# The adding stage of a two-layer metaformer: one block-diagonal product per pair of images, three sets of buffers, long runs, no loops

## The reference, cut to what matters

```python
probs = softmax(x @ gate_w.T + gate_b, axis=1)            # over the tokens of an image
vals, idx = top_k(probs.transpose(0, 2, 1), 8)            # 8 tokens per image and expert
topv, topi = vals.transpose(0, 2, 1), idx.transpose(0, 2, 1)
gathered = take_along_axis(x, topi.reshape(B, 8 * E)[:, :, None], axis=1).reshape(B, 8, E, D)
pooled = einsum('bked,bke->bed', gathered, topv)
h = gelu(einsum('ebd,edh->ebh', [pooled, 1], weight1))
out = einsum('ebh,eho->ebo', [h, 1], weight2)             # one row of 128 per image and expert
weighted = einsum('beo,bke->bkeo', out, topv)
outputs = zeros.at[b, topi].add(weighted)                 # added back to the chosen tokens
x = x + outputs
```

## Time and profile before

| | us |
|---|---|
| median of 3 executions | 14604.2 (14583.66 to 14649.89) |
| the profiled execution, its own time | 14537.58 |
| its span, first to last instruction | 14535.8 |
| mean granted TensorE clock in it | 0.810 of full speed |
| routing, experts, adding in the span | 11718 to 13396, to 13704, to 14535.8 |

### The profile page before, as it was taken

The page is one execution under the profiler, slowest core; times in us unless marked ns, Lnnn a source line. Parts: engine busy times, 40 slices in busy tenths (PEclk is TensorE's granted clock), DMA queues, the critical chain, the costliest instruction groups (busy, mean ns, idle before and its releaser), DMA issues. The chain is left out here.

```text
span 14535.8 us, 248087 instructions
## 1 busy us (share of the span) xinstructions
PE 11419.5 (79%) x87538; PEld 8744.4 (60%) x87538; DVE 11053.6 (76%) x22880; ACT 9833.3 (68%) x22679; POOL 4012.8 (28%) x3975
## 2 busy tenths in 40 slices
PE   7888888888888867777777777777777547776998
PEld 5666666666666645555555555555555235555888
DVE  6777777777777718999999999999999965554133
ACT  6888888888888846666666666667666567776100
POOL 5444444445444421212111211112121111211000
PEclk9999999999999967777777777777777677777555
DMA  3333333333333321111111111111111133333599
GB/s 69 86 81 82 81 82 87 76 90 73 90 77 86 75 61 41 53 53 53 51 47 52 53 53 53 51 46 53 53 52 40 23 84 94 99 90 89 172 316 309
DMA packets 1967708, 1189.72 MB, mean 82 GB/s; under 512 B 48853, under 2 KB 1900056, under 8 KB 1958436
## 3 DMA queue, kind: packets, MB, share of 16 engines
q1 hardware_dynamic: 1554148, 967.87, 26.3%
q10 hardware_dynamic: 408832, 205.55, 5.0%
q0 software_dynamic: 3648, 2.20, 0.1%
HBM read 708.85 MB, written 466.62 MB: 81 GB/s over the span
## 5 line engine op out<-in xcount | busy, mean ns | idle before, releaser
L1236 PEld LDWEIGHTS s_pW<-s_XU,s_vh 128*128 128x128 f32 x6272 | 1415.7, 261 | 1969.1 <-ACT s_XU L1107 1699.7
L1236 PE MATMUL s_pW<-s_XU,s_vh 128*128 128x64 f32 x6272 | 1493.2, 331 | 1071.4 <-ACT s_XU L1107 1071.4
L1107 ACT ACTIVATE s_XU<-s_pW,s_zb 128x64 f32<-128x64 f32 x3136 | 995.7, 318 | 1788.7 <-PE s_pW L1236 1738.1
L1265 PE MATMUL s_pG<-s_wg,s_XNT 128*128 128x384 f32 (+1 forms) x3200 | 1506.0, 559 | 37.5 <-ACT s_Z L1086 37.5
L832 POOL TENSOR_TENSOR s_rst<-s_var,s_epst 128x16 f32<-128x16 f32 (+1 forms) x100 | 141.7, 1417 | 3906.6 <-DVE s_var L79 3906.6
L408 ACT ACTIVATE KB<-pV,qkb 32x392 f32<-32x392 f32 x2048 | 1190.5, 581 | 25.0 <-PE pV L498 1.1
L248 POOL TENSOR_TENSOR SS<-SS,mx 128x784 f32<-128x784 f32 x512 | 769.5, 1503 | 804.8 <-DVE mx L341 804.6
L1203 PEld LDWEIGHTS s_pY<-s_hident,s_XU 128*128 128x128 f32 (+1 forms) x3200 | 752.2, 305 | 177.7 <-issue 129.6
L1711 PE MATMUL c_pS<-c_OX,c_Wm 64*112 64x128 f32 x3584 | 737.6, 420 | 91.1 <-DVE c_X L1727 76.6
L460 ACT ACTIVATE XH<-XR,nm,rs 112x128 f32<-112x128 f32 x1792 | 733.6, 485 | 92.1 <-POOL nm L267 83.6
L506 PE MATMUL pS<-KB,QT 128*64 128x196 f32 x8192 | 793.7, 336 | 0.0
(11 more groups left out here) (249 smaller groups left out, 31958.3 us busy)
## 6 DMA issues: line engine op xcount, KB each, us to landing
XL<-in_x_dram SPq DMA_DIRECT2D x64, 1568.0 KB, 12.4
XR<-in_x_dram SPq DMA_DIRECT2D x64, 1568.0 KB, 18.0
x_dram<-XR SPq DMA_DIRECT2D x64, 1568.0 KB, 8.1
xh_dram<-XH SPq DMA_DIRECT2D x64, 1568.0 KB, 8.1
r_X<-x_dram SPq DMA_DIRECT2D x64, 1568.0 KB, 14.2
c_X<-x_dram SPq DMA_DIRECT2D x64, 1568.0 KB, 19.4
out_dram<-c_X ACTq DMA_DIRECT2D x64, 1568.0 KB, 13.9
s_XQ<-xh_dram ACTq DMA_DIRECT2D x384, 256.0 KB, 2.8
```

The costliest lines, as they stand in the source:

```text
L1107: act.activation(XU[j % 2][:, t, :], pW[t // R % 2][:, B * (t % R):B * (t % R) + B], ACT.Tanh, bias=zb[:, 0:1], scale=0.5).then_inc(u_sb, 1)
L1236: pe.matmul(pW[t // R % 2][:, B * (t % R):B * (t % R) + B], vh[:], before, start=False, stop=True, skip_group_check=True).then_inc(z_ps, 1)
L1265: pe.matmul(pG[i % 3][0:tc, 0:3 * C], XNT[:, i, 0:tc], wg[:], start=True, stop=True).then_inc(g_ps, 1)
```

## The change

- In the adding stage both images of a pair share one product: 128 rows deep, 256 columns wide. OX becomes [128, 2, 128], with image 0's rows in the upper left block and image 1's in the lower right; the two other blocks are set to zero once, and the loads fill only their own blocks. A PSUM bank then holds two pieces of 112 tokens for both images, and VectorE's addition writes both images' X. There are 14 banks per pair, as before.
- X and Wm have three sets (NL = 3), allocated ahead of the experts. `load_pair` fills them; SP calls it in the experts' code at e = 8, 16 and 24 for pairs 0, 1 and 2, and afterwards in the adding stage. OX keeps two sets and is loaded there.
- Partition t now holds tokens t*NT + n, 28 tokens one after the other, so that a partition's run in DRAM is 28 x 512 = 14,336 bytes, in routing's loads, in the loads of the adding stage and in the stores of the output. The mask's order of tokens follows.
- Both stages are written out, without loops.
- Both images of a pair are stored when the whole pair is done.

```diff
@@ routing @@
-            with eng.Fori(0, (NP - 4) // 2) as i:
-                body(Image(i * 2 + 2, i + 1, 0), True, True, True)
-                body(Image(i * 2 + 3, i + 1, 1), True, True, True)
-            body(Image(NP - 2, NP // 2 - 1, 0), True, True, True)
+            for m in range(2, NP - 1):
+                body(Image(m, m // 2, m % 2), True, True, True)
...
-                                         .rearrange("a (n t) c -> t (a n) c", t=T)).then_inc(x_ld[n.par][o], 16)
+                                         .rearrange("a (t n) c -> t (a n) c", t=T)).then_inc(x_ld[n.par][o], 16)
@@ ahead of the experts @@
+        NL = 3
...
+        X = [sb(f"X{p}", [T, 2, NT, C]) for p in range(NL)]
+        Wm = [sb(f"Wm{p}", [P, S]) for p in range(NL)]
...
+        def load_pair(eng, m):
+            p = m % NL
+            eng.dma_start(Wm[p][:], wm_d[m]).then_inc(w_ld[p], 16)
+            for o in range(2):
+                eng.dma_start(X[p][:, o], x3_d[2 * m + o:2 * m + o + 1, :, :].rearrange("a (t n) c -> t (a n) c", t=T)
+                              ).then_inc(x_ld[p], 16)
@@ experts, SP, after the load of W2[e] @@
+                    if e in (8, 16, 24):
+                        load_pair(sp, e // 8 - 1)
@@ adding, SP @@
-                def body(m):
-                    wait(sp, s_ps, (m.idx - 1) * 2 * NG)
-                    sp.dma_start(Wm[m.par][:], ...)
-                    sp.dma_start(OX[m.par][:], ...)
-                    wait(sp, o_st[m.par], m.half * 32)
-                    for o in range(2):
-                        sp.dma_start(X[m.par][o][:], ...)
+                sp.wait_ge(zero, 1)
+                for m in range(NP):
+                    p = m % 2
+                    wait(sp, s_ps, (m - 1) * NU)
+                    for o in range(2):
+                        sp.dma_start(OX[p][E * o:E * o + E, o, :], ox_d[2 * m + o]).then_inc(ox_ld[p], 16)
+                    if m >= 1 and m + NL - 1 < NP:
+                        wait(sp, s_ps, m * NU)
+                        wait(sp, o_st[(m - 1) % NL], ((m - 1) // NL + 1) * 32)
+                        load_pair(sp, m + NL - 1)
@@ adding, ScalarE's queue @@
+                for m in range(NP):
+                    act.wait_ge(s_sb, m * NU + NU)
+                    for o in range(2):
+                        act.dma_start(out[2 * m + o:2 * m + o + 1, :, :].rearrange("a (t n) c -> t (a n) c", t=T),
+                                      X[m % NL][:, o]).then_inc(o_st[m % NL], 16)
@@ adding, TensorE @@
-                                w = pe.matmul(bank[0:T, C * t:C * t + C], Wm[m.par][E * o:E * o + E, T * n:T * n + T],
-                                              OX[m.par][E * o:E * o + E, :], start=True, stop=True)
+                for m in range(NP):
+                    pe.wait_ge(w_ld[m % NL], m // NL * 16 + 16)
+                    pe.wait_ge(ox_ld[m % 2], m // 2 * 32 + 32)
+                    for u in range(NU):
+                        i = m * NU + u
+                        wait(pe, s_sb, i - 3)
+                        for n in range(2):
+                            w = pe.matmul(pS[i % 4][0:T, 2 * C * n:2 * C * n + 2 * C],
+                                          Wm[m % NL][:, T * (2 * u + n):T * (2 * u + n) + T],
+                                          OX[m % 2][:].rearrange("p o c -> p (o c)"), start=True, stop=True)
+                        w.then_inc(s_ps, 1)
@@ adding, VectorE @@
+                for p in range(2):
+                    dve.memset(OX[p][0:E, 1, :], 0.0)
+                    w = dve.memset(OX[p][E:P, 0, :], 0.0)
+                w.then_inc(zero, 1)
+                for m in range(NP):
+                    dve.wait_ge(x_ld[m % NL], m // NL * 32 + 32)
+                    for u in range(NU):
+                        i = m * NU + u
+                        v = X[m % NL][:, :, 2 * u:2 * u + 2, :].rearrange("t o n c -> t n o c")
+                        dve.wait_ge(s_ps, i + 1)
+                        dve.tensor_tensor(v, pS[i % 4][0:T, :].rearrange("t (n o c) -> t n o c", n=2, o=2), v,
+                                          ALU.add).then_inc(s_sb, 1)
```

More of the change, by code:

```diff
@@ L1556, in expert_phase, with sb, sem @@
         NH4 = HID // P
+        NL = 3
+        def sb(name, shape, dt=F32):
+            return ctx.enter_context(nc.sbuf_tensor("c_" + name, shape, dt))
+        def sem(name):
+            return ctx.enter_context(nc.semaphore("c_" + name))
+        X = [sb(f"X{p}", [T, 2, NT, C]) for p in range(NL)]
+        Wm = [sb(f"Wm{p}", [P, S]) for p in range(NL)]
+        x_ld = [sem(f"x_ld{p}") for p in range(NL)]
+        w_ld = [sem(f"w_ld{p}") for p in range(NL)]
+        def load_pair(eng, m):
[4 more added lines that the diff above has]
+                              ).then_inc(x_ld[p], 16)
         with ExitStack() as ex:
@@ L1652, in sem @@
                 return sc.enter_context(nc.semaphore("c_" + name))
-            X = [[sb(f"X{p}{o}", [T, NT, C]) for o in range(2)] for p in range(2)]
-            Wm = [sb(f"Wm{p}", [P, S]) for p in range(2)]
-            OX = [sb(f"OX{p}", [P, C]) for p in range(2)]
+            OX = [sb(f"OX{p}", [P, 2, C]) for p in range(2)]
             pS = [ps(f"pS{a}", [P, 512]) for a in range(4)]
-            x_ld = [[sem(f"x_ld{p}{o}") for o in range(2)] for p in range(2)]
-            w_ld = [sem(f"w_ld{p}") for p in range(2)]
+            zero = sem("zero")
+            ox_ld = [sem(f"ox_ld{p}") for p in range(2)]
             s_ps = sem("s_ps"); s_sb = sem("s_sb")
[L1661 to L1669, removed]
+            o_st = [sem(f"o_st{p}") for p in range(NL)]
+            NU = NT // 2
             block = sc.enter_context(nc.Block())
@@ L1697, in _ @@
[L1697 to L1698 removed]
+                        act.dma_start(out[2 * m + o:2 * m + o + 1, :, :].rearrange("a (t n) c -> t (a n) c", t=T),
+                                      X[m % NL][:, o]).then_inc(o_st[m % NL], 16)
+                for p in range(NL):
+                    act.wait_ge(o_st[p], len(range(p, NP, NL)) * 32)
             @block.tensor
             def _(pe):
[L1702 to L1713 removed]
@@ L1715, in _ @@
-                each(body, pe)
+                for m in range(NP):
[9 more added lines that the diff above has]
+                        w.then_inc(s_ps, 1)
@@ L1717, in _ @@
             @block.vector
             def _(dve):
-                def body(m):
-                    for o in range(2):
-                        dve.wait_ge(x_ld[m.par][o], m.half * 16 + 16)
-                        for k in range(NG):
-                            i = (m.idx * 2 + o) * NG + k
-                            bank = pS[(o * NG + k) % 2 + 2 * m.par]
-                            v = X[m.par][o][:, GT * k:GT * k + GT, :].rearrange("t n c -> t (n c)")
-                            dve.wait_ge(s_ps, i + 1)
-                            dve.tensor_tensor(v, bank[0:T, :], v, ALU.add).then_inc(s_sb, 1)
@@ L1729, in _ @@
-                each(body, dve)
+                for p in range(2):
[10 more added lines that the diff above has]
+                                          ALU.add).then_inc(s_sb, 1)
```

18 lines of the change are left out of this document (removed).

## The result

| | before | after |
|---|---|---|
| median of 17 executions | 14608.2 us (14565.5 to 14649.9) | 14661.6 us (14625.7 to 14679.8) |
| ratio, 95% interval | | 1.0039 [1.0031, 1.0047] |
| profiled execution, its span | 14537.6, 14535.8 | 14660.2, 14658.4 |

The kernel is 0.4% slower. That lies within the 0.5% called no change ahead of the run, but with 17 executions on either side the interval excludes 1. It is 212 us over the forecast of 14450 and outside its range.

The account below looks back on a forecast made before the run. TensorE, transfers and the two-set ring were taken to bound the adding stage together, near 25.7 us per pair, with DMA the bound afterwards. 14604 - 161 (adding) + 6 (experts) + 0 (routing) = 14449, stated as 14450; range 14385 to 14575.

Parts of the forecast that it names:

- I take 401 for all of it: Adding stage: all transfers in long runs move at 401 GB/s, so two pairs take 40.4 us.
- Rival B: Adding stage: transfers stay at 345 GB/s because loads and stores share the engines; 47.5 us per two pairs, 14531; chance 0.10.
- I take 42 per two pairs: Adding stage: SP's queue chain takes 39 us, the DMA engines 40.4; interleaving imperfectly, 42 per two pairs.
- The products: Adding stage: 128-row depth brings TensorE's clock up; 12.3 us per pair, 14.8 if it starts low.
- the forecast of 671: Adding stage: start, first two bursts, 15 turns of 42 us and the end sum to 671 us against 832.
- Rival A: Adding stage: TensorE's clock stays at 0.50, bursts 23.9 us, stage 785, kernel 14564; chance 0.14.
- Loads among the experts: Experts: three early load points each make the following weights 2 us late, +6 us; bounds 0 and 12.
- Routing at 0: Routing: earlier X and removed loops cost 0; its rhythm may move +-40 us, none expected.
- Perhaps ten more slow pairs: Routing: the median's 66.6 us over the profiled execution of the kernel before comes from perhaps ten more slow pairs.
- C: Adding stage: long runs in both directions disturb each other; at 281 GB/s or less the kernel is 0.5% slower; chance 0.05.
- D: Routing and adding: instruction fetches of unrolled code stall TensorE, +189 us, kernel 14638; chance 0.03.
- The sum: Whole kernel: 14604 less 161 in the adding stage plus 6 in the experts gives 14449, stated as 14450.

Follow-up runs that it names:

- e6: Kernel after, with X loaded into 128 partitions of 28 tokens (1792 KB per image, rows not the right tokens): 14638.2 us in one execution, adding stage 824.
- e5: Kernel after, with each image of X loaded in two transfers, to partitions 0 to 63 and 64 to 111: ratio 1.0151, adding stage 983 us.
- e8: Kernel before, with 14,336-byte runs in routing's loads and the adding stage's loads and stores: ratio 0.9972, adding stage 793 us.
- e2: Kernel after, with X and the output moved in 512-byte pieces again: ratio 1.0088, adding stage 897 us.
- e3: Kernel after, with OX issued ahead of the next load_pair and its wait for a store: ratio 1.0015, adding stage 828 us.
- e7: Kernel before, with routing's pairs written out without a loop, nothing else changed: ratio 1.0003, routing 1753 us.
- e10: Kernel before, unedited, profiled a second time: 14603.8 us in one execution, routing 1743.
- e11: Kernel before, with pairs on 128 partitions, 64 x 64 quarter products, three sets, spread early loads, all OX loaded at the start: ratio 0.9849, adding stage 595 us.
- e12: Kernel after, with OX issued ahead as in e3 and the first three pairs' nine loads spread among the experts: ratio 0.9999, adding stage 814 us.
- e13: Kernel after, with the edits of e12 and the 128-partition loads of e6 together (rows not the right tokens): ratio 0.9916, adding stage 705 us.

## Why the prediction was wrong, step by step

Two steps failed: the bandwidth of the loads, and the time of the chain. The first alone would have made the stage some 770 us (41 + 15 x 48.5, an estimate from the rate below). The second held it at 824 even where the loads were fast (e6).

**"I take 401 for all of it."** It held for the stores (24.6 bytes per ns of one engine) and fell for the loads of X, 40% of all bytes: they go into 112 partitions, not into the 128 of the mask store from which the number came. A packet took 0.84 us; into 128 partitions with the same runs it took 0.535 (e6), and in two transfers of 64 and 48 partitions 1.12 (e5). Two pairs then need 9.78 MB / (16 x 19.0) + 6.42 / (16 x 24.6) = 32.2 + 16.3 = 48.5 us of all engines, not 40.4. Rival B had the right size (345 GB/s, 47.5 us) for another reason. The direction, long runs are faster, was right: e8 gains 39 to 43 us, e2 loses 56.

The mask has 128 rows, and the prediction did not ask what fewer partitions do. The Trainium skill (SBUF — State Buffer, Door 1: The DMA port swizzle) bears on it: partitions reach the DMA through 16 ports, and partitions 0 to 63 use only 8 of them. By it, as an estimate, the halves of e5 should go at half speed; the 1.12 us against 0.535 agree. Why a load into 112 partitions takes 1.6 times as long while a store out of them does not is not settled here.

**The chain, "I take 42 per two pairs".** The order on SP's queue was read rightly: OX lands 19.4 us after its issue, and the products begin when it has landed. The terms of the sum 8.0 + 1.2 + 12.3 + 1.2 + 1.3 + 14.8 = 39 were too small. In the turn from 14091.31 to 14144.11 the landing times give 13.8 for the burst, 0.8 to the issue of the stores, 11.9 for the stores (9.2 forecast) and 26.3 from the issue of the load until OX has landed (13.5 forecast): 52.8. Slow packets are not the main reason. With fast ones, in e6, the turn from 14026.90 is 13.9 + 0.8 + 12.2 + 24.8 = 51.7. There the load is in flight from 14053.83 to 14078.52, and the stores of the other pair from 14053.65 to 14071.40 (in after, 14117.82 to 14144.02 and 14125.81 to 14143.84). The forecast gave each transfer all the engines, but the two chains share them, and run close together instead of interleaving. Even at the right bandwidth the forecast of 671 would have been missed by some 150 (e6: 824). What keeps the two pairs together was not taken apart. Issuing OX ahead (e3) spread them, but did not end the wait for OX.

**The products.** Right. 128-row products brought the clock up, bursts of 13.8 to 15.3 us (14.8 forecast), the mean clock 0.76. Rival A is out. The 0.11 us per instruction was right, though 1.08 us for eight is 0.135: pairs at a clock of 1.00 throughout took 12.31 us (e6), and 12.3 was forecast. That it was the depth that brought the clock up was not shown alone, since the width of a product and the pauses between bursts changed with it. What failed is the value placed on it: TensorE's idle time grew by what its busy time lost.

**Loads among the experts.** Right place, wrong size: 32 us where 6 were summed and 12 was the bound. The sum took 401 GB/s there too. As an estimate, 5.34 MB at the 238 shown take 22.4 us, and 22.4 + 2 - 13.3 = 11 lies between the two smaller stalls of 8.1 and 8.4 and the 15.3 of the first; the difference between them is not explained. In e6 all three are shorter (5.5, 3.7, 4.0).

**Routing at 0.** Nearly right. Unrolling alone changes nothing (e7: 1.0003). With the whole change routing took 1763 in the profile, 20 us over e10, less than the 65 between two executions of the kernel before. Its rhythms are another mix, and the one of 61 us, in which the pooling products run at the lower clock, comes with the unrolling. What decides where in the pair the clock falls is open.

**"Perhaps ten more slow pairs"** for the 66.6 us between the profile and the median of before: e10 shows 20 instead of 12 of them, 2 of these of the 61-us kind. Right.

**Rivals C and D.** C asked for 281 GB/s or less; 291 came, through slow loads and idle engines, so a slower kernel came without C's mechanism: in e11 both directions at once reach 421. D is out for routing, where nearly all its cost was placed: the unrolled code in e7 costs nothing.

**The sum**: forecast 14604 - 161 + 6. Measured, against e10: + 5 (adding) + 33 (experts) + 20 (routing, not clear of its own scatter).

## What to carry to other kernels

A bandwidth read from one transfer holds for its shape: length of run, direction, and number of partitions. Where a load misses 128 partitions, price it from a load with the same partitions, or lay the data out over 128 first; here that was worth 109 us once the queue's order and the burst of loads among the experts were mended (e12 to e13).

When a stage has several bounds at nearly the same period (25.7 us per pair here, from TensorE, the transfers and the ring), relieving one returns little: the long runs alone gave 39 of 832 us. Sum each of them for the new kernel, with queue order included and with the transfers of the other chain in the same engines, before taking the longest.

Prefetch under another stage costs what its burst blocks on the queue. One load between two weights was hidden, three in a row stopped the experts for 8 to 15 us.

## What the hardware showed that was not expected

- Loads of 14,336-byte runs: 0.535 us a packet into 128 partitions (e6, e13), 0.84 into 112 (median; 0.74 to 0.86 in the adding stages of the other runs with one load per image), 1.12 when split into 64 and 48. Stores out of 112 took 0.535.
- Mixed loads and stores reach 421 GB/s over 550 us, 432 in a slice (e11). The page that the forecast drew on, the Trainium skill (DMA: Bandwidth & Descriptors, Where 436 GB/s comes from), names a ceiling of 435 for the ports and some 358 as a core's share of HBM; the first agrees, the second is exceeded with one core at work.
- TensorE's clock does not follow the depth of a product alone. 64-row products, one at a time and 89% busy, stayed at 0.50 for 832 us; two 64 x 64 quarters side by side, 70% busy, ran at 0.85 (e11).
- The same kernel's routing took 1678 and 1743 us in two executions (e10), because more of its pooling products ran at the lower clock: 477 us of them in the one, 527 in the other. A single profile can mislead by the size of the effect that is looked for.
